# GpSimd's queue: head-row store ahead of the rotary gather, and the gather held until the first full pair

## What is computed

```python
q_R = (c_Q @ W_QR.T).reshape(B, S, H, D_HR).transpose(0, 2, 1, 3)
q_R = rope(q_R, pos)
q = jnp.concatenate([q_C, q_R], axis=-1)
...
scores = jnp.einsum('bhqd,bhkd->bhqk', q, k)
scores = jnp.clip(scores, -80.0, 80.0)
scores = jnp.where(causal[None, None], scores, -jnp.inf)
weights = jax.nn.softmax(scores / jnp.sqrt(jnp.float32(d_qk)), axis=-1)
attn = jnp.einsum('bhqk,bhkd->bhqd', weights, v)
```

## Time and profile before

| | us |
|---|---|
| median of 3 runs | 1446.24 |
| lowest and highest | 1443.59, 1446.68 |
| the profiled execution, its own time | 1443.91 |
| its span, first to last instruction | 1442.4 |
| PE busy | 1379.0 (96%) |
| DVE busy | 1147.8 (80%) |
| ACT busy | 782.7 (54%) |
| POOL busy | 111.6 (8%) |
| granted TensorE clock, mean | 0.988 |

### The profile page before, as it was taken

How to read it: one execution, slowest core, us unless ns; L and a number is a source line. 1 busy time by engine, 2 the same in 40 slices (tenths; PEclk the granted TensorE clock), 3 DMA queues, 4 the chain that set the end, 5 groups by cost and what they waited for, 6 DMA issues and landing times. The chain is left out here.

```text
span 1442.4 us, 27855 instructions
## 1 busy us (share of the span) xinstructions
PE 1379.0 (96%) x9810; PEld 1128.1 (78%) x9810; DVE 1147.8 (80%) x1339; ACT 782.7 (54%) x861; POOL 111.6 (8%) x149
## 2 busy tenths in 40 slices
PE   7999689999999999999999999999999899599998
PEld 6888577788788788888788888887788788288887
DVE  7666478888889898989898898888788698576764
ACT  4233366675666666666666666667556566432221
POOL 0000121100110101010000100100000000112121
PEclk9999899999999999999999999999999999899999
DMA  8323666525434424242152421522412521345552
GB/s 302 119 84 126 162 183 176 184 85 153 125 96 141 127 84 127 84 127 84 55 152 59 122 89 55 146 65 60 127 55 84 193 60 53 118 133 168 168 175 88
DMA packets 112525, 172.77 MB, mean 120 GB/s; under 512 B 9288, under 2 KB 68968, under 8 KB 109672
## 3 DMA queue, kind: packets, MB, share of 16 engines
q1 hardware_dynamic: 98104, 111.10, 25.0%
q0 software_dynamic: 13552, 59.60, 14.1%
q10 hardware_dynamic: 832, 1.57, 0.5%
HBM read 123.75 MB, written 48.50 MB: 119 GB/s over the span
## 5 line engine op out<-in xcount | busy, mean ns | idle before, releaser
L1168 ACT CAST prob_h<-prob 128x1024 fp32r<-128x1024 f32 (+1 forms) x288 | 289.7, 1006 | 231.7 <-DVE prob L1252 184.3
L1021 PE MATMUL score_ps<-q_h,key_slot 64*128 64x512 f32 x1792 | 359.7, 394 | 12.1 <-DMA key_slot<-keys 11.2
L1162 ACT ACTIVATE prob<-score_ps 128x1024 f32<-128x1024 f32 (+1 forms) x288 | 281.8, 979 | 163.8 <-PE score_ps L1021 114.2
L1270 DVE TENSOR_TENSOR prob_l<-prob,prob_h 128x1024 fp32r<-128x1024 f32 (+1 forms) x288 | 335.9, 1166 | 39.7 <-ACT prob_h L1168 38.3
L1043 PE MATMUL out_ps<-prob_h,value_slot 64*128 64x512 f32 (+1 forms) x1792 | 340.6, 375 | 0.2
L1265 DVE TENSOR_TENSOR total<-total,prob 128x1024 f32<-128x1024 f32 (+1 forms) x256 | 294.9, 1152 | 0.0
L1252 DVE TENSOR_SCALAR prob<-prob 128x1024 f32<-128x1024 f32 x224 | 155.1, 693 | 82.7 <-ACT prob L1162 82.7
L1021 PEld LDWEIGHTS score_ps<-q_h,key_slot 64*128 64x128 f32 x1792 | 172.8, 185 | 51.1 <-issue 9.0
L1043 PEld LDWEIGHTS out_ps<-prob_h,value_slot 64*128 64x128 f32 x1792 | 172.6, 185 | 35.4 <-DVE prob_l L1270 2.3
L1021 PE MATMUL score_ps<-q_l,key_slot 64*128 64x512 f32 x896 | 178.6, 391 | 0.0
L1021 PE MATMUL score_ps<-rot_hh,key_slot 64*128 64x512 f32 x896 | 178.3, 390 | 0.0
(11 more groups left out here) (203 smaller groups left out, 1986.4 us busy)
## 6 DMA issues: line engine op xcount, KB each, us to landing
key_slot<-keys SPq DMA_DIRECT2D x144, 256.0 KB, 2.7
value_slot<-values SPq DMA_DIRECT2D x144, 128.0 KB, 2.0
rows<-heads_rows SPq DMA_DIRECT2D x32, 512.0 KB, 5.7
rot_hh<-turned POOLq DMA_DIRECT2D x30, 512.0 KB, 6.1
heads_rows<-head_rows POOLq DMA_DIRECT2D x15, 1024.0 KB, 9.9
turned<-rot_hl POOLq DMA_DIRECT2D x14, 1024.0 KB, 4.6
rot_l<-turned POOLq DMA_DIRECT2D x30, 256.0 KB, 7.7
wo<-in_w_o POOLq DMA_DIRECT2D x1, 4096.0 KB, 13.5
```

What stands on the lines that cost most here:

```text
L1021: mm = pe.matmul(score_ps[:, half, c * 512:(c + 1) * 512], keys_of[ROWS[r], :], moving[par][ROWS[r], half * HW + c * 512:half * HW + (c + ...
L1162: nc.scalar.activation(prob[half][:, 0:width], score_ps[:, half, 0:width], ACT.Exp, scale=QK_SCALE).then_inc(exp_done, 1)
L1168: nc.scalar.copy(prob_h[half][:, 0:width], prob[half][:, 0:width]).then_inc(high_done, 1)
L1270: nc.vector.tensor_tensor(p_l, p, p_h, ALU.subtract).then_inc(split, 1)
```

## The change

In `during`, the store of unit n - 1 is issued first. The gather for unit n + 1 comes second, and in units 2 to 13 (those with FULL pairs and with a unit two ahead to turn) it waits for `r_step` to reach 4n + 2, that is for both additions of DVE at the end of F0, and no longer for `q_scored`. In units 0, 1 and 14 it still waits for `q_scored`, now by a constant. The scatter stays last. No transfer is added, removed or resized.

```diff
-            queries = pool.alloc_register("queries")
-            pool.reg_mov(queries, 3)
+            adds = pool.alloc_register("adds")
+            pool.reg_mov(adds, 10)
...
-                if has_next:
-
-                    since(pool, passed, 16 * n)
-                    pool.wait_ge(q_scored, queries)
-                    pool.reg_add(queries, queries, 2)
-                    gather(pool, n + 1, 1 - par, scattered)
                 if not first:
                     store(n - 1)
+                if has_next:
+
+                    since(pool, passed, 16 * n)
+                    if has_full and has_second:
+                        pool.wait_ge(r_step, adds)
+                        pool.reg_add(adds, adds, 4)
+                    else:
+                        pool.wait_ge(q_scored, 2 * n + 3)
+                    gather(pool, n + 1, 1 - par, scattered)
                 if has_second:
                     pool.wait_ge(r_step, 4 * n + 4)
...
-            during(0, 0, first=True)
-            during(1, 1)
+            during(0, 0, first=True, has_full=False)
+            during(1, 1, has_full=False)
```

More of the change, by code:

```diff
@@ L909, in store, with during @@
                                sums[0:P:32, :]).then_inc(sums_stored, 16)
-            queries = pool.alloc_register("queries")
-            pool.reg_mov(queries, 3)
-            def during(n, par, first=False, has_next=True, has_second=True):
+            adds = pool.alloc_register("adds")
+            pool.reg_mov(adds, 10)
+            def during(n, par, first=False, has_next=True, has_second=True, has_full=True):
+                if not first:
+                    store(n - 1)
                 if has_next:
                     since(pool, passed, 16 * n)
-                    pool.wait_ge(q_scored, queries)
-                    pool.reg_add(queries, queries, 2)
+                    if has_full and has_second:
[3 more added lines that the diff above has]
+                        pool.wait_ge(q_scored, 2 * n + 3)
                     gather(pool, n + 1, 1 - par, scattered)
-                if not first:
-                    store(n - 1)
                 if has_second:
```

## The result

The changed kernel takes 1517.8 us (median of 6 runs, 1514.7 to 1520.4), the kernel before 1445.5 us (6 runs): the ratio is 1.050, 95% interval 1.049 to 1.052. It is slower by 72 us. The forecast was 1483 (1462 to 1500), slower by 37 us: right in sign, right in most of the places, and half of the size.

A forecast was written before the change was run, and what follows sets the result against it. PE, busy 96% of the span, was taken to bound the kernel. Terms 3.1 + 16.4 + 3.9 + 19.0 - 5.5 + 0.3 = +37.2 us on 1446.2 gave 1483.4, forecast 1483 us, range 1462 to 1500.

The forecast's parts named there:

- The bound, the release and the deadline: PE bounds; gather released at DVE's second addition; slack 2.0 us to unit 3's CORNER, 9.0 us to unit 8's F3.
- The two late CORNERs: CORNERs behind units 2 and 3: PE waits 8.2 us each, 16.4 us, bounds 7.2 to 9, plus 3.6 us for the clock.
- The new wait of 1.9 us at F3: Units 4 to 13: F3's keys land behind the gather, 1.9 us each, 19.0 us in ten; bounds 0 to 3.4 us.
- unit 0's 10.2 us: Length of unit 0's gather with no store behind it, first issue to landing, taken as every late gather's length.
- key loads get past the gather: Rival, chance 0.22: F3 in units 4 to 13 doesn't wait, some 2 us more at late CORNERs; 1466 us.
- I leave the drop out: At F3 of units 4 to 13, no clock drop counted behind 1.9 us waits, nearer 1.77 (no drop) than 2.75 (drop).
- the rival with 0.15: Clock falls at F3 too: ten waits a little over 2 us, 1.5 us more each, +52.2 us, 1498 us; chance 0.15.
- Removed: -5.5: Nine PE waits for keys at F1 in units 3 to 13 go, winning 5.5 us.
- Unit 1 and unit 14: Stores first, gather last: unit 1 +3.1 us and 0.3 us for the longer wait behind it; unit 14 +0.3 us.
- a fixed total of 12.6 us: Unit 1: time from first issue to last landing before the change, kept for the new order, from 191.34 to 203.9.
- The quick gather: Rival, chance 0.03: with the store out of its way the gather lands in about 4.6 us; change 0, 1446 us.
- the gather elsewhere: Rival, chance 0.02: `r_step` already reached, gather follows the store in the CORNER pair, F1 keeps its waits; 1450 us.

The follow-up runs named there:

- at_late: The changed kernel with the gather of units 2 to 13 released by `begun` 2n + 2, at the LATE pair, instead of `r_step`: 1472.1 us, 1.019.
- store_late: The kernel before with stores of head rows and sums held back until `r_step` reaches 4n + 2 in units 2 to 13, gather unmoved: 1445.6 us, 1.000.
- weights_only: The kernel before with only unit 15's 4 MB load of the output weights cut into four pieces: 1436.6 us against 1444.7, 0.993.
- clip_later: The changed kernel with DVE in F1 running the add of the pair before first and the clip second: 1524.5 us, 1.054.
- first_add: The changed kernel with the gather released at the first of DVE's two additions (`r_step` 4n + 1) instead of the second: 1500.4 us, 1.040.

## Why the prediction was wrong

By units, the span's 73.8 us stand so (from the starts of the CORNER pairs in the two profiles; the slow start of unit 4's CORNER is counted with unit 3):

| part | predicted | measured |
|---|---|---|
| ahead of unit 1 | 0 | 0.8 |
| unit 1, up to unit 2's CORNER | 3.4 | 5.3 |
| units 2 and 3, CORNER waits and clock | 20.0 | 23.0 |
| units 4 to 13 | 13.5 | 40.7 |
| unit 14 | 0.3 | 2.9 |
| behind it | 0 | 1.1 |

**The bound, the release and the deadline** were right: PE pays at unit 2's CORNER, at those of units 3 and 4 and at F3 of ten units, and beside these 1.4 us at unit 14's F1 and 0.9 us at unit 15's F0. The two late CORNERs came out within 3 us, but their waits of 10.29 and 9.67 us lie above the bounds of 7.2 to 9, by the same two terms as the F3 waits below.

**Units 4 to 13 are the failure**, 27 us short of what was measured. Three terms of the sum carry it: the F3 waits (12.5 us), the clock behind them (9.6 us) and the waits that were to be removed (5.1 us).

*The new wait of 1.9 us at F3* measured 3.15 us on average (31.5 us in ten). That alone is within the bounds of 0 to 3.4 us; with the clock, 4.1 us a unit, it is not. I took the issue to follow the release at once; it takes 0.8 us. And I took unit 0's 10.2 us for the gather; here it takes 10.6 to 11.6 us, and SP's value and key loads for the next pairs, 384 KB, are served among it. Against these the key load lands only 0.2 us behind the gather in unit 8, and not 0.7. Busy shares and rates for unit 8, late in the gather (columns as in rows 7):

```profile
555.50:560.50 5.00, 2.71 (x24) 1.90 (x20) 5.00 (x6) 2.96 (x4) 0.73 (x1) 1.00 1.04 234
```

The engines are full. Which queue their packets were of (q0 is POOL's, q1 SP's: packets, MB, share of the 16 engines), from 552.0 to 555.5 and then from 555.5 to 561 us:

```profile
q0 software_dynamic: 227, 0.86, 102.4%
...
q0 software_dynamic: 283, 0.96, 68.8%
q1 hardware_dynamic: 288, 0.39, 33.9%
```

The key load is issued at 552.0, and none of SP's packets starts before 555.5; then both share the engines, and the gather ends at 560.9, the key load at 561.2. So the rival "key loads get past the gather" was wrong about the outcome. They get in among it, late, and lengthen it without landing before it. Nor does this load get a share of the engines as soon as it is issued: it had no packet for 3.5 us and needed 9.2 us, where the one for the same pair needed 2.8 us before.

*"I leave the drop out"*: the clock fell behind six of the ten F3 waits. Two stretches right behind waits of 3.40 and 3.06 us (length, PE busy, granted clock, DMA share, GB/s):

```profile
499.10:502.50 3.40, 3.40 (x30) 1.00 0.76 296
562.40:565.70 3.30, 3.30 (x20) 0.50 0.44 166
```

The first kept a granted clock of 1.00, the second ran at 0.50, and F3 of unit 8 took 8.6 us instead of 7.0. Six times 1.6 us are 9.6 us. This was the rival with 0.15, and its ground was the one I named, a wait that comes out longer than 1.9 us. The reason for leaving the drop out, that 1.9 lies nearer 1.77 than 2.75, doesn't hold either: 3.40 us went without a drop here, and in at_late 1.76 us had one. What the prediction calls 1.2 GHz is the granted clock of 0.50 in the earlier trace rows, a share of full speed; no run shows a frequency.

*"Removed: -5.5"* measured about -0.4 us (40.7 - 31.5 - 9.6). The step that failed is that the sum took as a gain all that PE waits there. A wait of PE is worth its length only if PE would have run on; here DVE, busy without a pause, held PE in the next two pairs. store_late shows it by its time and by the lengths of its pairs. And the 5.5 us were one execution's; that of weights_only has 1.3.

**Unit 1 and unit 14** were mis-sized for one reason. I counted a small delay of the start and a fixed total of 12.6 us for the 2.5 MB. In unit 1 they start 0.6 us later than I took and need 14.0 us (192.67 to 206.65). In unit 14 they start 0.5 us later in the unit than before and need 13.3 us instead of 12.6, and the F1 wait is 2.50 us for 1.06; the other 1.5 us are the clock, which falls behind this wait (length, PE busy, granted clock, DMA share, GB/s):

```profile
1091.60:1094.60 3.00, 3.00 (x14) 0.50 0.43 132
```

Why the same transfers need longer in this order in these two units stays open. SP's loads don't explain it: as much of them, 360 to 380 KB, is served among the 2.5 MB in the kernel before.

**The quick gather** and **the gather elsewhere** fell: no late gather landed in less than 10.6 us, and POOL's idle time ahead of `rot_hh` was ended by DVE's L1239 twelve times.

What stays open: why a wait of 2.56 us brought the clock down here and one of 3.40 us didn't; the runs show both and no rule. Open, too, is why SP's packets start only 3.4 to 4.5 us behind the issue of F3's keys in the ten units.

## What to carry to other kernels

When a transfer is moved in time, its length must be compared with the time to every deadline behind it, not only its own consumer's: here the gather was wanted a unit later, and the load queued behind it was wanted at the next pair. Before counting a removed wait as a gain, see what else holds the engine in the same stretch, and whether the wait is there in a second execution. Where a transfer is larger than the gap between two regular loads, cut it: 4 MB in four pieces won 8 us, and it was a wait that the list of PE's waits showed as its longest in a FULL pair from the start.

## What the runs showed of the hardware

- In POOL's loop the first DMA is issued 0.7 to 0.8 us after the instruction that releases it has ended, be it PE's, ACT's or DVE's, and about 0.3 us where the code is straight and the wait is for a constant. In the loop: 0.78 us behind DVE's addition (unit 8, changed kernel, 549.06 to 549.84), 0.70 us behind ACT's copy (unit 7, changed kernel, 468.46 to 469.16), 0.77 us behind PE's scores (unit 7, kernel before, 427.69 to 428.46). In straight code: 0.30 us behind ACT's copy (unit 1, changed kernel, 192.37 to 192.67). No run takes the loop and the register apart.
- Two DMA issues of POOL took 1.72 us instead of 1.27 where DVE's clip began inside the first, 0.27 us into it (clip_later, 554.68). Where the clip had begun 0.27 us before the first issue, the two took 1.27 us (first_add, 540.59). The first case shows 0.45 us more, the second none; why, no run shows.
- The cost of a late gather wasn't linear here: 0.6 us earlier took 1.25 us on average off an F3 wait (31.5 us in ten to 18.8), and the clock fell behind three of these waits instead of six (first_add).
- A 256 KB load issued on SP's queue 2.1 us behind a 1.5 MB gather of POOL's took 9.2 us (unit 8 with the change) where it took 2.8 us before.
- Waits of PE of 2.56, 3.06, 3.28, 3.48, 3.48 and 3.56 us were followed within 1.5 us by a stretch at a granted clock of 0.50, those of 2.59, 2.96, 3.12 and 3.40 us were not: the 7 us behind each are at 1.00 (the ten F3 waits of the changed kernel).
